# The last outputs of a Mamba, attention and gated-unit block: additions of two batches on GpSimd, the last batch stored in halves, one norm issued earlier

## The reference

```python
x = x + mamba_and_mlp(layernorm(x))
x = x + gated_unit(layernorm(x))
x = x + attention(layernorm(x))
x = x + gated_unit(layernorm(x))        # the same weights again
```

```python
def step(c, xt):
    ft = sigmoid(xt @ wf.T + c @ uf.T + bf)
    it = sigmoid(xt @ wi.T + c @ ui.T + bi)
    gt = tanh(xt @ wc.T + c @ uc.T + bc)
    return ft * c + it * gt, None
c_final, _ = lax.scan(step, c0, x)
h = tanh(einsum('tbi,oi->tbo', x, wo) + c_final @ uo.T + bo)
```

## Time and profile before

| | |
|---|---|
| median of 3 runs | 1515.91 us (1515.25 to 1517.03) |
| the profiled execution's own time | 1515.18 us |
| its span, first to last instruction | 1513.4 us |
| busy share of the span | PE 90%, DVE 74%, ACT 57%, POOL 42% |
| mean granted TensorE clock | 0.954 of full speed |

### The profile page before, as it was taken

The page is one execution under the profiler, slowest core; times in us unless marked ns, Lnnn a source line. Parts: engine busy times, 40 slices in busy tenths (PEclk is TensorE's granted clock), DMA queues, the critical chain, the costliest instruction groups (busy, mean ns, idle before and its releaser), DMA issues.

```text
span 1513.4 us, 17340 instructions
## 1 busy us (share of the span) xinstructions
PE 1366.0 (90%) x5574; PEld 665.2 (44%) x5574; DVE 1127.2 (74%) x1810; ACT 861.5 (57%) x1494; POOL 642.4 (42%) x386
## 2 busy tenths in 40 slices
PE   6427799999999998999878899999999999999998
PEld 2103445455555545455432344444435454444444
DVE  4889888989999898941288887777868677777235
ACT  6656776777677673531225656556465656555633
POOL 2596969796969684822133222122131312100000
PEclk9757999999999999999968999999999999999999
DMA  4843343444352534112073433333331432330145
GB/s 138 287 145 113 126 154 127 140 138 140 112 155 93 173 115 138 28 42 70 0 188 92 92 79 91 76 88 85 72 97 46 102 83 59 70 70 3 39 142 168
DMA packets 94106, 158.04 MB, mean 104 GB/s; under 512 B 8720, under 2 KB 74832, under 8 KB 91088
## 3 DMA queue, kind: packets, MB, share of 16 engines
q1 hardware_dynamic: 94016, 156.94, 35.6%
HBM read 110.91 MB, written 46.01 MB: 104 GB/s over the span
## 4 chain that ended last, share of the span: by engine, by line
PE 62%; DVE 15%; issue 10%; POOL 6%; ACT 5%; DMA 2%; SPq 0%; POOLq 0%; ACTq 0%; DVEq 0%
PE psum L1071 23%; PE psum L2099 8%; PE psum L2033 7%; PE psum L2007 6%; PE psum L2022 5%; DVE mx L1469 5%; PE psum L1975 4%; DVE psum L567 3%; PE psum L1123 2%; POOL hb L1004 2%; PE psum L1096 1%; DVE middle L550 1%; DVE stats L1445 1%; ACT back L797 1%; PE psum L2194 1%
## 5 line engine op out<-in xcount | busy, mean ns | idle before, releaser
L1725 ACT ACTIVATE pw<-psum 128x512 f32<-128x512 f32 x512 | 302.0, 598 | 272.9 <-PE psum L2022 269.9
L1469 DVE TENSOR_REDUCE mx<-psum 128x1 f32<-128x512 f32 x512 | 343.2, 686 | 144.8 <-PE psum L2007 143.7
L1004 POOL TENSOR_TENSOR hb<-ddb,bcb 128x1024 f32<-128x1024 f32 x127 | 296.8, 2360 | 68.1 <-DVE middle L550 54.0
L567 DVE TENSOR_TENSOR_SCAN psum<-psum,hb 128x512 f32<-128x512 f32 x224 | 261.6, 1213 | 22.9 <-POOL hb L1004 13.7
L2007 PE MATMUL psum<-kp,qp 96*128 96x512 bf16 x512 | 202.6, 400 | 22.6 <-DVE mx L1469 18.6
L793 ACT ACTIVATE psum<-ddb,A_neg 128x512 f32<-128x512 f32 x256 | 165.4, 682 | 83.8 <-DVE hb L570 67.1
L2022 PE MATMUL psum<-qp,kp 99*128 99x512 bf16 x512 | 196.6, 385 | 5.3 <-ACT pw L1725 4.6
L1904 POOL TENSOR_TENSOR rstd<-rstd,neg_half 128x4 f32<-128x4 f32 x15 | 15.3, 1018 | 402.1 <-DVE rstd L1454 402.1
L570 DVE TENSOR_TENSOR hb<-psum,bcb 128x1024 f32<-128x1024 f32 x112 | 137.2, 1225 | 3.9
L2033 PE MATMUL psum<-pw,v_sb 128*32 128x512 f32 x1024 | 124.9, 605 | 0.5 <-ACT pw L1725 0.5
L1071 PE MATMUL psum<-back,w 128*128 128x512 f32 x256 | 114.9, 600 | 4.0 <-ACT back L809 1.9
(11 more groups left out here) (217 smaller groups left out, 2087.2 us busy)
## 6 DMA issues: line engine op xcount, KB each, us to landing
ddb<-dd SPq DMA_DIRECT2D x64, 512.0 KB, 6.5
bcb<-bc SPq DMA_DIRECT2D x32, 512.0 KB, 6.7
parts<-parts_sb SPq DMA_DIRECT2D x96, 128.0 KB
qp<-parts SPq DMA_DIRECT2D x30, 256.0 KB, 7.6
dd<-dd_out SPq DMA_DIRECT2D x7, 1024.0 KB, 5.2
kp<-parts SPq DMA_DIRECT2D x15, 384.0 KB, 4.5
x_back<-x_dram SPq DMA_DIRECT2D x9, 512.0 KB, 8.0
qp<-parts SPq DMA_DIRECT2D x34, 128.0 KB, 6.1
```

Of the source, the lines that this page charges most:

```text
L567: e.tensor_tensor_scan(to[:, g, :], a[:, g, :], h[:, g, :], 0.0, ALU.mult, ALU.add).then_inc(scan_ok, 1)
L1004: e.tensor_tensor(hb[n % NHB], ddb[k % NSLOT][:, 1:2, :].to_broadcast([P, 2, L]), bcb[q][:, 0, :, :], ALU.mult).then_inc(bx_ok, 2 if n == ...
L1469: used.up(e.tensor_reduce(mx[u % 2][:, n:n + 1], score_bank(used.n), AXIS.X, ALU.max))
L1725: e.activation(pw[n % NPW], bank(5 + n % 2), ACT.Exp, scale=HD ** -0.5).then_inc(exp_ok, 1)
```

## The change

It has two parts, which share nothing.

At the end, the sums with `cuo` and the final additions of batches 4 and 5 move to GpSimd, which runs nothing there before: four instructions of 128x1024, two sums, then two additions, each addition behind its tanh. With that batch 5 no longer goes through TensorE, VectorE has one sum and two additions fewer, ScalarE takes the tanh of batches 4, 5 and 6 one after the other from SBUF, and SyncE stores in the order 0, 1, 2, 4, 3, 5, 6. The last batch's tanh, addition and store are released in two halves of two token tiles each.

In the first phase, ScalarE issues the norm of batch 7 ahead of the forget gate's tanh of batch 6.

```diff
--- before.py
+++ after.py
@@ -315,6 +315,7 @@
         set_v, set_k = sem("set_v"), sem("set_k")
         max_pe, max_dve, nm_ok, nm_sent, nm_in = sem("max_pe"), sem("max_dve"), sem("nm_ok"), sem("nm_sent"), [sem(f"nm_in{i}") for i in range(3)]
         qk_first = sem("qk_first")
+        out_pool, outp_ok = sem("out_pool"), sem("outp_ok")
         st_pe, exp_ok, pv_pe, ot_ok = (sem(n) for n in ("st_pe", "exp_ok", "pv_pe", "ot_ok"))
         g_var, g_rstd, xr2_ok, p2_ok, c2_new = (sem(n) for n in ("g_var", "g_rstd", "xr2_ok", "p2_ok", "c2_new"))
         x3_sent, xwo2_sent = [sem(f"x3_sent{i}") for i in range(2)], [sem(f"xwo2_sent{i}") for i in range(2)]
@@ -929,6 +930,8 @@
                         front_square(i + 2)
                     if u == 13 and front:
                         front_rms(i + 2)
+                    if u == 15 and i == NB:
+                        gate_apply(i - 1)
                     if u == 15 and gate:
                         gate_f(i - 2)
                     if u == 15 and i == NB + 1:
@@ -936,7 +939,7 @@
                         e.activation(tok(G2)[:, 0:2, :], halves(ring("xwo", i - 2, 0)), ACT.Copy).then_inc(r_act, 1)
                     if u == 15 and front:
                         front_turned(i + 2, (0,))
-                    if u == 15 and back:
+                    if u == 15 and back and i != NB:
                         gate_apply(i - 1)
                     if u == 15 and front:
                         front_turned(i + 2, (1,))
@@ -1420,12 +1423,15 @@
                 e.dma_start(out_x[b], rows_of(x3_dram[b])).then_inc(out_in[b], 16)
                 e.wait_ge(xwo2_sent[b % 2], 16 * (b // 2 + 1))
                 e.dma_start(out_xwo[b], rows_of(xwo2_dram[b])).then_inc(out_in[b], 16)
-            for b in range(NB):
-                e.wait_ge(out_ok, b + 1)
-                src = out_x[b] if b < NB - 1 else x2[b % 4]
-                e.dma_start(out[b].rearrange("(t p) d -> p t d", p=P), src).then_inc(out_sent[b % 2], 16)
-            for i in range(2):
-                e.wait_ge(out_sent[i], 16 * NB // 2)
+            for b, done, n in ((0, out_ok, 1), (1, out_ok, 2), (2, out_ok, 3), (4, outp_ok, 1), (3, out_ok, 4), (5, outp_ok, 2), (6, out_ok, 5)):
+                e.wait_ge(done, n)
+                e.dma_start(out[b].rearrange("(t p) d -> p t d", p=P), out_x[b]).then_inc(out_sent[b % 2], 16)
+            for k in range(2):
+                half = slice(2 * k, 2 * k + 2)
+                e.wait_ge(out_ok, 6 + k)
+                e.dma_start(out[NB - 1].rearrange("(t p) d -> p t d", p=P)[:, half, :], x2[(NB - 1) % 4][:, half, :]).then_inc(out_sent[1], 16)
+            e.wait_ge(out_sent[0], 16 * NB // 2)
+            e.wait_ge(out_sent[1], 16 * (NB // 2 + 1))
 
 
         def dve_second(e, own):
@@ -1705,15 +1711,22 @@
 
             def out_add(b):
                 e.wait_ge(out_tanh, b + 1)
-                x, y = (out_x[b], out_xwo[b]) if b < last else (x2[b % 4], tok(H2))
-                e.tensor_tensor(x, x, y, ALU.add).then_inc(out_ok, 1)
+                e.tensor_tensor(out_x[b], out_x[b], out_xwo[b], ALU.add).then_inc(out_ok, 1)
+
+            def last_add(k):
+                half = slice(2 * k, 2 * k + 2)
+                e.wait_ge(out_tanh, NB + k)
+                e.tensor_tensor(x2[last % 4][:, half, :], x2[last % 4][:, half, :], tok(H2)[:, half, :], ALU.add).then_inc(out_ok, 1)
 
             out_sum(0)
             out_sum(2)
-            for b in range(NB):
-                if b % 2 == 1 and b + 3 < NB:
-                    out_sum(b + 3)
+            out_add(0)
+            out_add(1)
+            out_sum(6)
+            for b in (2, 3, 6):
                 out_add(b)
+            for k in range(2):
+                last_add(k)
 
 
         def act_second(e, own):
@@ -1871,16 +1884,30 @@
                         misc_done(e, ("gf", last, 1))
                         e.activation(feat(dst)[:, f, :], misc(("gf", last, 1)), ACT.Tanh, bias=bias(f), scale=scale).then_inc(m2_act, 1)
 
-            for b in range(0, NB, 2):
-                e.wait_ge(out_dve, b // 2 + 1)
+            def out_one(b):
                 e.activation(out_xwo[b], out_xwo[b], ACT.Tanh).then_inc(out_tanh, 1)
-                if b + 1 == last:
-                    e.wait_ge(xwo2_sent[(last - 1) % 2], 16 * ((last - 1) // 2 + 1))
-                y = out_xwo[b + 1] if b + 1 < last else tok(H2)
+
+            def out_halves(b, n, y):
+
                 for u in range(2):
-                    e.wait_ge(out_pe, b + u + 1)
+                    e.wait_ge(out_pe, 2 * n + u + 1)
                     ins = e.activation(y[:, 2 * u:2 * u + 2, :], halves(bank(OUT_BANKS[b // 2][u])), ACT.Tanh)
-                ins.then_inc(out_tanh, 1)
+                    if b == last or u == 1:
+                        ins.then_inc(out_tanh, 1)
+
+            e.wait_ge(out_dve, 1)
+            out_one(0)
+            out_halves(1, 0, out_xwo[1])
+            e.wait_ge(out_dve, 2)
+            out_one(2)
+            out_halves(3, 1, out_xwo[3])
+            for b in (4, 5):
+                e.wait_ge(out_pool, b - 3)
+                out_one(b)
+            e.wait_ge(out_dve, 3)
+            out_one(6)
+            e.wait_ge(xwo2_sent[(last - 1) % 2], 16 * ((last - 1) // 2 + 1))
+            out_halves(last, 2, tok(H2))
 
 
         def pool_second(e, own):
@@ -1962,6 +1989,14 @@
                     sub(b + 2, 0, 2)
 
             power(1, g_var, NB, g_rstd)
+
+            e.wait_ge(cuo_ok, 4)
+            for b in (4, 5):
+                e.wait_ge(out_in[b], 32)
+                e.tensor_tensor(out_xwo[b], out_xwo[b], cuo, ALU.add).then_inc(out_pool, 1)
+            for b in (4, 5):
+                e.wait_ge(out_tanh, b + 1)
+                e.tensor_tensor(out_x[b], out_x[b], out_xwo[b], ALU.add).then_inc(outp_ok, 1)
 
 
         def pe_second(e):
@@ -2220,11 +2255,7 @@
                 out_state_term(1, u)
             for u in range(2):
                 out_state_term(3, u)
-            e.wait_ge(out_in[5], 32)
             e.wait_ge(cuo_ok, 4)
-            for u in range(2):
-                out_xwo_term(5, u)
-                out_state_term(5, u)
             for u in range(2):
                 to = bank(OUT_BANKS[3][u])
                 e.matmul(to, ident, cuo[:, 2 * u:2 * u + 2, :].rearrange("p t d -> p (t d)"), start=True, stop=False)
```

## The result

| | before | after |
|---|---|---|
| median of 4 runs each | 1516.47 us (1515.25 to 1518.09) | 1524.62 us (1523.00 to 1525.26) |
| profiled execution, own time / span | 1515.18 / 1513.4 us | 1523.00 / 1521.2 us |
| mean granted TensorE clock | 0.954 | 0.952 |

The changed kernel is slower: 1.0050 times the time of before, 95% interval 1.0038 to 1.0062, or 8.2 us between the medians. That is beyond the upper end of the predicted range, 1524.0, by 0.6 us.

The account below looks back on a forecast made before the run. The end was taken as bound by the full DMA store queue behind TensorE's chain, set by the fourth store's issue. 1515.18 + 7.5 (end) - 1.05 (norm) = 1521.65, median 1522.4 us; range 1517.5 to 1524.0.

Parts of the forecast that it names:

- the sum: Whole kernel: 1515.18 + 7.5 - 1.05 = 1521.65 us for the profiled execution, 0.73 below the median, so 1522.4.
- the norm: First phase: moved norm starts L1173 1.05 us earlier, passed on whole as a gain; bounds 0 and 4.0.
- Exclusion: Output part: GpSimd and VectorE, both reading two SBUF inputs, block each other for whole instructions, making two queues one.
- Order of service: Output part: no row shows who goes first when both wait; alternating costs 7.9 us, VectorE keeping its turn 7.1.
- The hand-made chain: Output part, turn by turn: addition 2 ends 1510.12, GpSimd 1509.02, last half 1513.6; stores end 7.9 us later.
- The end's term: Output part and stores: 7.5 us slower, taken between 7.1 and 7.9 for the two orders of service.
- No exclusion: Rival, output part: both engines run freely, 0.3 us gained there, 1.3 with the norm, 1514.6 us; chance 0.10.
- The clock that stays up: Rival, first phase: TensorE's clock does not fall at the norm, 3.0 us more come back, 1519.4 us; chance 0.35.
- The stores not the limit: Rival, output part: engines exclude each other but the end follows the last addition, 4.2 us later, 1519.1 us; chance 0.03.

Follow-up runs that it names:

- e3: Changed kernel with one operand of VectorE's whole sums and additions in the output part read from idle PSUM banks; 1516.38 us against 1516.98, ratio 0.9993.
- e1: Kernel before with only the norm of batch 7 issued ahead of the forget gate's tanh; 1517.10 us against 1516.98, ratio 0.9996.
- e4: Changed kernel with SyncE's stores in the order in which the batches are ready; 1521.44 us, ratio 1.0027.
- e15: Kernel before with only the norm moved ahead of the tanh, measured once more; 1516.50 us against 1516.95, ratio 1.0000.
- e11: Kernel before with the norm moved, VectorE's additions in store order, first and last batch in halves, GpSimd's subtractions whole; 1514.65 us against 1516.14, ratio 0.9990.
- e9: Kernel before with the norm moved and each GpSimd subtraction of the second phase issued as two halves; 1514.17 us against 1516.14, ratio 0.9988.
- e12: Kernel before with the norm moved, GpSimd's second-phase subtractions in halves, and stores fed earlier by VectorE's reordered additions; 1513.13 us against 1516.14, ratio 0.9981.
- e13: The whole changed kernel with GpSimd's second-phase subtractions in halves; 1521.57 us against 1516.95 of before, ratio 1.0037.
- e10: Kernel before with only GpSimd's second-phase subtractions in halves, norm and outputs untouched; 1516.30 us against 1516.14, ratio 0.9996.
- e14: Changed kernel's output part without the norm's move, GpSimd's second-phase subtractions in halves; 1521.92 us against 1516.95 of before, ratio 1.0044.
- e5: Kernel before with the norm moved and one second-phase GpSimd subtraction waiting for VectorE's chain of maxima; 1515.61 us against 1516.01, ratio 0.9997.
- e8: Kernel before with VectorE's output work in the order the stores need, first and last batch in halves; 1515.48 us against 1516.01, ratio 0.9991.

## Why the prediction was wrong

The direction and nearly every row of the end were right; the range missed by 0.6 us. That the miss is so small says little, and so does that it is one. The range ended 8.1 us above the 1515.91 of before; the medians measured differ by 8.2 us, the ratio gives 7.6, and its interval 5.8 to 9.4. What failed is a term of the sum, the norm.

*Exclusion* was right. e3 shows it: the same instructions with one operand from PSUM cost 8.2 us less. The sizes held too: 2.2 and 1.1 us from the other's end. VectorE's instruction took 1.08 us from GpSimd's recorded end against 1.21 alone, and GpSimd's 2.21 from VectorE's end against 2.35, so each gains 0.1 us there, as far as GpSimd's recorded times, which are rough, can tell. The 115 ns of delay that the Trainium skill gives in "SBUF — State Buffer", section "A bandwidth-pool intuition that's wrong", there for work of GpSimd behind one of VectorE, are not seen in these rows. The blocking for the whole instruction is.

*Order of service*: open in the prediction, now seen. In eight turns of eight the engine that had waited went next, so the two alternate. The closest of these was 0.15 us: GpSimd's addition of batch 4 starts at 1502.16, VectorE's next at 1502.31, and GpSimd goes first. At 0.08 us it is the other way round: in the earlier trace rows GpSimd's row starts at 1286.93 and VectorE's L1592 at 1287.01, and yet VectorE goes first. So the starts don't tell the order to 0.1 us. The hand-made chain gave batch 2's addition for 1510.12; its store was issued at 1510.12. The chain had one turn wrong: it let VectorE go on with addition 1 before GpSimd's addition of batch 4, so GpSimd was through at 1507.88 instead of 1509.02. The last work, due at 1513.6, ended at 1513.57 all the same. The DMA engines, due to run dry at 1520.3, were full until after 1520.0 and half busy (0.54) from there to 1520.5.

*The end's term*: I took 7.5, between 7.1 and 7.9, and it measured 7.77 (29.10 less 21.33 in the ledger). The chain's own 7.9 was nearer than the compromise with an order of service that did not occur.

*The norm, the step that failed.* "Everything behind it is one chain into the second phase, so I pass it on whole": 1.05 us, with no row from behind the first phase to carry it. The start itself was exact: L1173 starts 0.95 earlier in a trace that is 0.1 late at 700 us, so 1.05. With the shorter stretch of half clock, 3.4 us instead of 6.8, the gain at 730 us was even 2.2 to 2.3, in every trace with the norm. What arrives at 1490 us is less than 0.2 in five traces of six (after, e1, e3, e4, e15) and 0.4 in the sixth (e11). The term was thus 0.0 and not 1.05.

Two losses are seen on the way. The first is the clock's. Its part of the gain, 1.2 us, comes from 3.4 us less at 1.2 GHz at the norm. In all six traces 3.4 us more follow within 80 us (17.1 instead of 13.7 from 798 on, in e11 20.5 instead of 17.1 from 775 on), and the sum of 54.6 us up to 1490 is that of before. Between 730 and 842 us 0.7 to 0.9 of the lead go (1.4 in e11). Why the clock makes up for it so exactly is not shown.

The second is the wait under GpSimd. From 842 to 866 the five (all but e11) gain 2.6 us; before has its clock at half for 3.4 us at 842 and again at 862, they have not. All five have both collisions, a TensorE wait of 2.3 us and 6.8 us of half clock after it, and lose 4 us between 866 and 880. With halves of GpSimd's subtraction the change from 700 to 1490, before rounding, is -1.7 to -1.9 with the norm (e9, e12, e13) and -0.6 and -1.0 without (e10, e14), so about 1.0 us of the norm's gain lasts. That is the size of what was predicted, 1.05; but the two traces without the norm differ by 0.4 between themselves, so the close agreement is in part luck. That VectorE's wait under GpSimd is part of the cause is shown by that, in the traces if not in the medians; whether it is all of it isn't. A further 1.6 us or so goes between 880 and 905 us in all three, where the granted clock is at 0.50 for 3.4 us from 897 us on. And e11, which has no second collision, was down to 0.8 us of lead by 842 and 0.4 by 866. Why it goes there stays open.

*The sum.* 1515.18 + 7.77 + 0.0 is 1522.95, and the profiled execution took 1523.00. The median of the runs lies 1.6 above that one, where I had counted 0.73; I put this down to the chance of the first phase (the column at 700, -0.2 to 2.9), which no step about the change could give; it is not shown, since the other executions have no trace. The error of 2.2 us in the median is thus 1.05 for the norm, 0.3 for the end, 0.9 for this offset.

*The rivals.* No exclusion (0.10): excluded by the rows; its gain was small as forecast, 0.6 us in e3's output part where I had 0.3. The clock that stays up (0.35): it fell for half as long, 1.2 of the 3.0 us came, and none of it was there at the end. The stores not the limit (0.03): excluded by the 9.2 us of full queue, and by e4, where only SyncE's order changed and 3.05 us came back.

## What to carry to other kernels

Before giving an idle GpSimd some elementwise work, look whether VectorE's work at that time takes all its inputs from SBUF. If it does, the two take turns, and the sum of their times, 1.08 and 2.21 us per addition here, is what it costs; one operand in PSUM removes that. Not only additions of two tiles are held up: here also a cast of 32x128 (2.2 instead of 0.21 us) and two TENSOR_SCALAR of 128x256. A store queue in program order must be reordered along with the work, which was 40% of this loss. A lead won early in a long program is worth only what the phases behind it let through: measure it at several points of the trace, not at the end, together with the time that the clock spent at either level. Where it vanishes, shortening the instruction that others wait under did better here than adding a wait (from 700 to 1490 us, e9 -1.9 and e5 -0.5).

The best version here is e12, with the norm, the subtractions in halves and the stores fed earlier by VectorE alone: 1513.13 us against 1516.14, 3.0 us faster than before (0.9981, 0.9972 to 0.9990) and some 11 below the change.

## What was unexpected of the hardware

- A subtraction of 128x1024 that GpSimd issues as two of 128x512 took 2.27 to 2.29 us instead of 2.13: 0.15 us for the split. (The row of e9 is above.) VectorE's waits under it became 1.0 us shorter near 862 and near 1030 us; in the kernel before only the second reached TensorE, with 0.9 us (e10 and e14 between 905 and 1490).
- SyncE's issue of a store took 0.37 us in before, even at 1509.43, in the middle of the stretch with a DMA share of 1.00. In the changed kernel, where seven follow one another, it rose from 0.37 over 0.51 to 1.37 us. So busy DMA engines alone don't lengthen it; what does is not shown. It cost nothing here, since the engines stayed full:

```profile
1511.26 0.88 SPq L1428 DMA_DIRECT2D out_dram<-out_x  x1
...
1513.53 1.31 SPq L1428 DMA_DIRECT2D out_dram<-out_x  x1
...
1514.88 1.37 SPq L1432 DMA_DIRECT2D out_dram<-x  x1
```

- Executions differ in when the first phase reaches 700 us, by 3.1 us over 17 traces in which the code up to there is the same. Of the six that are 1.7 to 2.9 us late, five have 85.3 to 88.7 us at 1.2 GHz before that point; the other eleven have 78.5 to 81.9. From there on, traces of the same code agree to about 0.4 us, except e8, whose second phase is that of before and takes 2.9 us longer.
- Time at 1.2 GHz between 700 and 1490 us was 54.6 us in fourteen traces of seventeen, although its stretches lay differently. Saving a stretch early did not save it in the sum.
